# Second attention: later keys set to zero on GpSimd behind the exponential, early weight splits on VectorE

## What is computed

```python
attn = einsum('bhqd,bhkd->bhqk', q, k) / sqrt(16) + alibi
attn = where(causal, attn, finfo(float32).min)
p = softmax(attn, axis=-1)
out = einsum('bhqk,bhkd->bhqd', p, v)
x = layernorm(x + out @ Wo + bo)
```

## Time and profile before

| | us |
|---|---|
| median of 3 runs | 1631.5 |
| lowest, highest | 1629.63, 1633.35 |
| span of the profiled execution | 1649.7 |
| TensorE busy in it | 1550.0 (94%) |
| VectorE busy | 1101.0 (67%) |
| ScalarE busy | 930.4 (56%) |
| GpSimd busy | 636.6 (39%) |
| second attention's pairs, from the first exponential's table to the last value group | 556.0 to 686.2 and 1368.2 to 1498.6 |

### The profile page before, as it was taken

One profiled execution on the slowest core, in us unless ns is written; L12 is line 12 of the kernel. 1 busy time (PEld: TensorE's weight loads), 2 busy tenths in 40 slices (PEclk: granted clock), 3 DMA queues, 4 the chain that ended last, 5 costly groups with the idle time before them and its releaser, 6 DMA issues.

```text
span 1649.7 us, 30985 instructions
## 1 busy us (share of the span) xinstructions
PE 1550.0 (94%) x10774; PEld 1341.8 (81%) x10774; DVE 1101.0 (67%) x2705; ACT 930.4 (56%) x2054; POOL 636.6 (39%) x582
## 2 busy tenths in 40 slices
PE   8999999999899999999898999999998999998985
PEld 7888889888888677688787898898988876776885
DVE  6767667677645787574577676676766377874655
ACT  5666565665444577543556655656654346775353
POOL 1635444554461101252535354444654510031631
PEclk9999999999999999999999999999999999999998
DMA  3110000020120422034220200000201113322132
GB/s 132 46 52 17 27 1 16 25 91 1 40 69 10 75 51 61 21 120 137 76 96 1 77 18 26 16 7 18 91 1 58 50 36 61 60 60 101 56 126 106
DMA packets 48195, 88.03 MB, mean 53 GB/s; under 512 B 9600, under 2 KB 30480, under 8 KB 46928
## 3 DMA queue, kind: packets, MB, share of 16 engines
q1 hardware_dynamic: 43552, 75.28, 15.9%
q0 software_dynamic: 3744, 10.26, 1.7%
q10 hardware_dynamic: 768, 0.79, 0.2%
HBM read 60.18 MB, written 19.76 MB: 48 GB/s over the span
## 4 chain that ended last, share of the span: by engine, by line
PE 66%; DVE 15%; ACT 9%; issue 6%; POOL 3%; ACTq 1%; DMA 0%; DVEq 0%; POOLq 0%; SPq 0%
PE ps L408 16%; PE ps L410 15%; PE ps L409 15%; PE ps L1193 4%; PE ps L1210 4%; PE ps L1153 4%; ACT E L1407 3%; DVE nmax L1806 3%; PE ps L916 2%; POOL E L2274 2%; ACT PT_h L1389 1%; DVE On L1724 1%; DVE PT_l L1781 1%; PE ps L1189 1%; PE ps L844 1%
## 5 line engine op out<-in xcount | busy, mean ns | idle before, releaser
L1407 ACT ACTIVATE E<-ps,nmax 128x128 f32<-128x128 f32 (+7 forms) x256 | 188.9, 741 | 208.5 <-DVE nmax L1806 208.2
L2271 POOL TENSOR_SCALAR E<-E,mixc 128x128 f32<-128x128 f32 (+7 forms) x128 | 97.0, 758 | 396.2 <-DVE mixc L1774 396.2
L1806 DVE TENSOR_REDUCE nmax<-ps 128x1 f32<-128x128 f32 (+7 forms) x256 | 183.3, 749 | 12.7 <-PE ps L893 12.5
L1568 ACT ACTIVATE PT<-ps 128x512 f32<-128x512 f32 x288 | 155.0, 601 | 58.8 <-PE ps L1193 57.7
L2274 POOL TENSOR_TENSOR E<-E 128x128 f32<-128x128 f32 (+7 forms) x128 | 182.4, 1425 | 10.7
L408 PE MATMUL ps<-V_h,PT_h 128*128 128x256 f32 x576 | 168.0, 292 | 0.5 <-DVE O L1786 0.5
L409 PE MATMUL ps<-V_l,PT_h 128*128 128x256 f32 x576 | 163.8, 284 | 0.0
L410 PE MATMUL ps<-V_h,PT_l 128*128 128x256 f32 x576 | 163.6, 284 | 0.0
L408 PE MATMUL ps<-K_h,Q_h 128*128 128x512 f32 (+3 forms) x384 | 147.4, 384 | 8.7 <-ACT E L1407 5.4
L2026 DVE CUSTOM_DVE_ANT_0 masked<-ps,causal 128x128 bf16<-128x128 f32 (+3 forms) x256 | 111.1, 487 | 39.5 <-PE ps L1153 37.8
L1781 DVE TENSOR_TENSOR PT_l<-ps,PT_h 128x128 fp32r<-128x128 f32 (+7 forms) x128 | 96.7, 756 | 60.7 <-ACT PT_h L1389 60.0
(11 more groups left out here) (265 smaller groups left out, 4622.8 us busy)
## 6 DMA issues: line engine op xcount, KB each, us to landing
Wa_raw<-in_wa SPq DMA_DIRECT2D x8, 1024.0 KB, 6.0
Fw_raw<-in_fa SPq DMA_DIRECT2D x32, 256.0 KB, 2.6
E_raw<-in_fe SPq DMA_DIRECT2D x8, 768.0 KB, 7.5
xs<-in_xs SPq DMA_DIRECT2D x2, 2967.0 KB, 12.6
Wo_raw<-in_wo SPq DMA_DIRECT2D x8, 512.0 KB, 3.5
yg<-ys SPq DMA_DIRECT2D x8, 512.0 KB, 5.2
xg<-xs SPq DMA_DIRECT2D x6, 645.0 KB, 8.1
KS<-QK_h SPq DMA_DIRECT2D x56, 64.0 KB
```

Source lines behind the costliest of these rows:

```text
L1407: nc.scalar.activation(e[:, 0:w], ps[m][:, 0:w], ACT.Exp, bias=nmax[:, s % 4, m:m + 1], accum_out=lsum[:, s % 4, m:m + 1]).then_inc(exp_do ...
L1568: nc.scalar.activation(PT[:, at:at + HALF], bank1(RING1 + n % RING1), ACT.Exp, scale=SCALE1).then_inc(t_used, 1)
L1806: nc.vector.tensor_reduce(nmax[:, s % 4, m:m + 1], ps[m][:, 0:(q_tile(s, last) + 1) * P], AX.X, ALU.max, negate=True).then_inc(nmax_ready[ ...
```

## The change

The mask products go, for all 160 diagonal pieces. The exponential gets a bias of -40 from a new column `shift` (so that the unmasked scores of later keys do not overflow; it cancels in the division by the sum). Behind each exponential of a diagonal piece GpSimd sets the later keys to zero in place, `affine_select` over one or two 128x128 blocks, and counts `p_cut`; the value groups wait for it besides. GpSimd's addition of X's bias is cut into eight, one in each pair behind the cut of t0. The early splits go to VectorE, both steps, behind the output of pair 6 inside the last pair. Three semaphores of `max_cols` become one.

```diff
+SHIFT1 = 40.0
...
+        shift = sb("shift", [P, 1], F32, s)
...
+    CUT = [j for j in range(TURNED1) if diagonals(j)]
...
-                if diagonal:
-                    blocks = bank.rearrange("p (k c) -> p k c", c=P)[:, diagonal[0]:diagonal[-1] + 1:max(1, diagonal[-1])]
-                    nc.tensor.matmul(blocks, mask_r[:], ident_r[:].unsqueeze(1).to_broadcast([P, len(diagonal), P]),
-                                     start=True, stop=True, skip_group_check=True)
...
+                pe.wait_ge(p_cut, len(CUT) * G + sum(j <= max(v_needs(k)) for j in CUT))
...
-                                         scale=SCALE1).then_inc(t_used, 1)
+                                         scale=SCALE1, bias=shift[:]).then_inc(t_used, 1)
...
+                    if p == PAIRS1 - 1:
+                        for c in EARLY:
+                            early_split(b, c)
+
+        def early_split(b, c):
+
+            dve.wait_ge(fw_in[c % 2], CHUNKS * 16 * b + (c + 2 - c % 2) * 16)
+            if c == EARLY[0]:
+                dve.wait_ge(a_ready, PIECES1 * PAIRS1 * (b + 1))
+            nc.vector.tensor_copy(Fw_h[c % FW_RING][:], Fw_raw[c % 2][:]).then_inc(fw_early, 1)
+            dve.wait_ge(fw_early, FW_RING * b + c - EARLY[0] + 1)
+            nc.vector.tensor_tensor(Fw_l[c % FW_RING][:], Fw_raw[c % 2][:], Fw_h[c % FW_RING][:].bitcast(F32),
+                                    ALU.subtract).then_inc(fw_lo, 1)
...
+        def add_tile_bias(t):
+            ins = nc.gpsimd.tensor_tensor(X[:, t, 0:HID], X[:, t, 0:HID], rows_bc[:, 1, :], ALU.add)
+            if t == NT - 1:
+                ins.then_inc(xb_done, 1)
+
+        def cut_future(G, p, j):
+
+            blocks = diagonals(j)
+            at = pt_slot(p, j)
+            part = PT[:, at:at + HALF].rearrange("p (k c) -> p k c", c=P)[:, blocks[0]:blocks[-1] + 1:max(1, blocks[-1])]
+            pool.wait_ge(t_used, TURNED1 * G + j + 1 + RING1)
+            nc.gpsimd.affine_select(part, part, pattern=[[0, len(blocks)], [1, P]], compare_op=ALU.is_ge, fill=0.0, base=0,
+                                    channel_multiplier=-1).then_inc(p_cut, 1)
...
-            pool.wait_ge(xt_ps, LN_B // 2 * b + 12)
-            add_bias(1)
-            pool.wait_ge(a_ready, PIECES1 * (PAIRS1 * b + PAIRS1 - 1) + 1)
-            for c in EARLY:
-                ffn_split(b, c)
+            for p in range(PAIRS1):
+                for j in CUT:
+                    cut_future(PAIRS1 * b + p, p, j)
+                    if j == CUT[0]:
+                        if p == 0:
+                            pool.wait_ge(xt_ps, LN_B // 2 * b + 12)
+                        add_tile_bias(p)
```

More of the change, by code:

```diff
@@ L386, in program @@
     a_used = sem("a_used")
-    nm_both = sem("nm_both")
-    nm_hi = sem("nm_hi")
+    nm_step = sem("nm_step")
     nm_lo = sem("nm_lo")
@@ L393, in program @@
     t_used = sem("t_used")
+    p_cut = sem("p_cut")
     pv1_done = sem("pv1_done")
@@ L568, in program, with diagonals @@
             at += z - a
+    def diagonals(j):
+        starts = itertools.accumulate([z - a for n, kb, a, z in T_PIECES[j]], initial=0)
+        return [at // P for at, (n, kb, a, z) in zip(starts, T_PIECES[j]) if a == kb * P]
+    CUT = [j for j in range(TURNED1) if diagonals(j)]
     def v_rounds(c):
@@ L612, in program @@
     EPS_SET, IDENT_R, MASK_R, LAM_SUMS, LAM_SET, W2_SUMMED = 1, 2, 6, 8, 9, 12
-    FILLS = 9
+    FILLS = 10
     block = ctx.enter_context(nc.Block())
@@ L1185, in score_piece_t @@
                 starts = list(itertools.accumulate([z - a for n, kb, a, z in T_PIECES[j]], initial=0))
-                diagonal = [at // P for at, (n, kb, a, z) in zip(starts, T_PIECES[j]) if a == kb * P]
-                if diagonal:
-                    blocks = bank.rearrange("p (k c) -> p k c", c=P)[:, diagonal[0]:diagonal[-1] + 1:max(1, diagonal[-1])]
-                    nc.tensor.matmul(blocks, mask_r[:], ident_r[:].unsqueeze(1).to_broadcast([P, len(diagonal), P]),
-                                     start=True, stop=True, skip_group_check=True)
                 short_first = sorted(zip(starts, T_PIECES[j]), key=lambda part: part[1][3] - part[1][2])
@@ L1193, in score_piece_t @@
                     mm = nc.tensor.matmul(bank[:, at:at + z - a], KS[:, p % K_PAIRS, tile(kb)],
-                                          QS[:, 2 * (p % Q_PAIRS) + n, a:z], start=not diagonal and k == 0, stop=True,
+                                          QS[:, 2 * (p % Q_PAIRS) + n, a:z], start=k == 0, stop=True,
                                           skip_group_check=True)
@@ L2038, in max_cols @@
             if h == 1:
-                nc.vector.tensor_tensor(nmax1[:, tiles], nmax1_part[:, 0], nmax1_part[:, 1], ALU.min).then_inc(nm_both, 1)
-                dve.wait_ge(nm_both, G + 1)
+                nc.vector.tensor_tensor(nmax1[:, tiles], nmax1_part[:, 0], nmax1_part[:, 1], ALU.min).then_inc(nm_step, 1)
+                dve.wait_ge(nm_step, 3 * G + 2)
             high, low = (nmax1_cols[:, tiles, MAX_ROW + i::SLOT1] for i in range(2))
-            nc.vector.tensor_copy(high, nmax1[:, tiles]).then_inc(nm_hi, 1)
-            dve.wait_ge(nm_hi, 2 * G + h + 1)
+            nc.vector.tensor_copy(high, nmax1[:, tiles]).then_inc(nm_step, 1)
+            dve.wait_ge(nm_step, 3 * G + 2 * h + 1)
             nc.vector.tensor_tensor(low, nmax1[:, tiles], high.bitcast(F32), ALU.subtract).then_inc(nm_lo, 1)
@@ L2288, in ffn_split @@
         def ffn_split(b, c):
[L2289 to L2295, removed]
+            pool.wait_ge(fw_hi, (CHUNKS - FW_RING) * b + c + 1)
             low(Fw_l[c % FW_RING][:], Fw_raw[c % 2][:], Fw_h[c % FW_RING][:]).then_inc(fw_lo, 1)
@@ L2330, in ffn0 @@
                         nc.gpsimd.memset(*fill).then_inc(filled, 1)
+                    nc.gpsimd.memset(shift[:], -SHIFT1).then_inc(filled, 1)
         def split_wb(it):
```

## The result

The changed kernel takes 1637.86 us (median of 5 runs, 1637.27 to 1641.68) beside 1631.52 for the kernel before (5 runs, 1629.63 to 1633.35): 1.0038 times as long, 95% interval 1.0027 to 1.0049, so 6.3 us or 0.4% slower. The forecast was 1631.8 and no change; the range held it. The profiled execution is the slowest of the five, 1641.68 us with a span of 1639.9.

A forecast was written before the change was run, and what follows sets the result against it. TensorE, busy without a gap in full pairs, was taken as the bound. Per attention +0.42 (first pair) - 2.40 (six full) + 2.11 (last) = +0.13 us, twice +0.3: 1631.8 us, range 1624 to 1643.

The forecast's parts named there:

- Products removed: TensorE's mask products, ten per pair at 0.117 us: at most 18.7 us won over 16 pairs.
- The column: ScalarE's exponential with a bias column read from memory: 0.09 us more each, in length (0.69) and spacing (0.58).
- The column costs the exponentials nothing: Faster rival: the bias column is free, -7.2 us, 1624.6; chance 0.20, shared with more slack behind the cut.
- The cut: GpSimd's zeroing of later keys: 0.42 us for one block, 0.62 for two.
- The cut is dear: Slower rival: GpSimd's slow cuts queue and hold value groups, 1639 at middle value; chance 0.34, shared with late splits.
- v1 to v2: Second to third value group of a full pair: longer route through exponentials and cut, 3.60 us against 3.18, loses 0.42.
- the rest of the pair: From the third value group to the next pair's second: seven mask products go, 0.82 us won, no new wait.
- A full pair: Each of six full pairs per attention gains 0.40 us, 2.4 us together; 16.18 us a pair.
- First pair: Bound by VectorE's maxima up to its first value group: wins nothing, loses 0.42 us before its third.
- Last pair: TensorE waits directly for exponentials and cuts before the third and fourth value groups: 2.11 us lost.
- Early splits at nothing: Weight splits on VectorE in the last pair, covered by 0.9 us before the last output, cost nothing.
- the rival on contention: VectorE, slowed beside GpSimd's cuts, comes late to the last output: up to 2.9 us, twice, 1637.6; within the slower 0.34.

The follow-up runs named there:

- e8: The change without the exponential's bias column (shift put into VectorE's maxima), with neither cuts nor mask products, later keys left in; 0.9956 of the kernel before.
- e1: The kernel before, mask products kept, with only the shift column added as bias of the exponentials; 1.0017 of the kernel before.
- e2: The change with the exponential free of the bias column, the shift put into VectorE's maxima instead; 0.9991 of the kernel before.
- e3: The change with the five early weight splits back on GpSimd, behind its last cut; 1.0041 of the kernel before.
- e4: The kernel before with only the early weight splits moved to VectorE in the last pair; 1.0003 of the kernel before.
- the control: The changed kernel run again unaltered, beside three variants of it; 1.0058 of the kernel before.
- e9: The change, column kept, with mask products again for pieces 13 and 14 of all pairs and for the whole last pair; 0.9964 of the kernel before.
- e6: The change without the bias column, mask products again for pieces 13 and 14 and the whole last pair; 0.9949 of the kernel before.

## Why the prediction was right in its sum and wrong in its outcome

**Products removed**, 0.117 us each: e8 has 0.101 in a full pair. Sixteen such pairs would give 16 us, not 18.7, and since the first and last pairs win less, e8 got 11.4.

**The column**, 0.09 in length and in spacing: right (697 ns; four in 2.42 us, predicted 2.43). "The column costs the exponentials nothing" is refuted by e1 and e2; "ScalarE: Activation LUTs" of the Trainium skill (What ACT_TABLE_LOAD costs) is borne out in the 93 ns of a pointer operand (697 against 601 here) and nearly so in the overlap of neighbours (0.11 us before, 0.12 now). As the overlap stays, the spacing grows by as much as the length, and e2 wins 0.33 us a pair. That rival's price, 7.2 us, is met by e2's work (-7.3); its median came down by only 2.5, for the clock.

**The cut**, 0.42 and 0.62: 0.29 and 0.41 undisturbed. "The cut is dear" is refuted. **v1 to v2** loses 0.34 us (3.97 to 4.31 between starts) where 0.42 was forecast, and the rest of the pair gains 0.71, not 0.82; TensorE waits for GpSimd before v2 in every pair, as written. **A full pair** takes 16.21 us against 16.18: two errors of 0.1 us that cancel.

**First pair** +0.45, forecast +0.42; in batch 1 1.06 more, with half clock ahead of v0.

**Last pair** +2.11 forecast (at its own prices cut_17 would queue 0.04 behind cut_16, which this sum leaves out). e3's batch 0, where nothing runs beside the cuts, has +2.10, in part by errors that cancel: the cuts were priced too high and what comes before them too low. In the change it is +3.33 and +2.12.

**Early splits at nothing**: right for the splits (e4), the last output and the loads; wrong for what they do to their neighbour. Of the rival on contention the mechanism was there but with the other engine paying: not VectorE comes late, GpSimd's cuts do, by 1.2 us in one batch of two. The text had named that and not priced it. That this rival's 1637.6 is close to the 1637.86 measured is chance: the output never waited for VectorE.

**The step that failed** is one that the sum does not have: it took TensorE's clock as full, because the pairs before show 1.00. Taken apart, the 6.17 us are: 1.1 of waits and work at full clock (0.45 + 0.47 - 2.18 - 1.86 + 2 x 2.10), 1.2 of stretched cuts, and 3.8 at half clock (2.78 behind v3, 1.06 in the first pair of batch 1). The 0.7 before the feed-forward, at half clock too, comes on top. Of the 1.1 the forecast had 0.3; the six pairs won 2.18 and 1.86 and not 2.40. Over the runs the same stands in the clock: work +0.4 us (+0.4 in the control) and 0.0042 of clock, which is 6.9 us of 1637. That the work matches the forecast's +0.3 so well is partly luck, since it puts kernels with spells too low.

So "160 products go and the time stays" was right to 1 us at full clock, with the stretched cuts set aside. The range held the outcome, but not by its own reasons: its upper part was made for a dear cut, and the cut was cheap. The forecast saw a wait of 1.3 us more before v2 and 0.8 before v3 in the last pair, and counted them at their length; behind them TensorE ran at 1.2 GHz for up to 10 us, in six last pairs of eight.

## What to carry to other kernels

Move masking off the bottleneck engine only for pieces whose consumer comes later than the longer route, and keep the old form where a consumer waits directly, above all in the last round of a loop that has nothing else to overlap: here that turned +0.6% into -0.4% on one chip (the control and e9), and without the column gave -0.5% (e6). Compare the mean granted clock of many runs before and after: where it has moved, span times clock tells roughly whether work or clock made the difference, and puts the work too low where TensorE waits at half clock. A longer wait on TensorE can cost more than its length, and an engine given work "in idle time" must also be checked against the engine that it slows down there.

## What was not expected of the hardware

The program alone does not settle where the clock falls: the same last pair is at full clock in one batch and at half in the other, and e2's runs span 0.988 to 0.996. With TensorE idle 1.05 to 1.44 us before v2 and 1.55 to 2.58 before v3 it fell in six last pairs of eight, with 0.3 to 0.5 and 0.9 to 1.1 in one of twelve, and with e2's 0.95 to 1.21 and 1.56 in none of two. With idle products in those gaps it fell in none of two, though elsewhere in the program it still did.

The cut of 128 columns (0.29 us) is shorter than GpSimd's one-input operation on as many (0.37), so the allowance that the forecast made for the comparison with the position was not needed. Two of 256 columns stretched from 0.82 to 1.82 us beside VectorE's cast and two-input subtraction; in e3, beside GpSimd's subtractions, VectorE's four operations stretched from 1.39 to 3.42 instead: the first of them, recorded from 694.38, ended at 696.43, 0.15 after GpSimd's subtraction (694.48 to 696.28).
